# GpSimd widens the quantised rows and multiplies a third lent tile in the gate stage of a quantised feed-forward block

## The reference, cut to what matters

```
def _act_fake_quant(x, clip_factor):
    scale = jax.nn.sigmoid(clip_factor) * jnp.max(jnp.abs(x)) / QMAX
    return jnp.clip(_ste_round(x / scale), -QMAX - 1.0, QMAX) * scale
...
xq = _act_fake_quant(x, clip_x[0])
gate = jnp.einsum('bsh,ih->bsi', xq, _weight_fake_quant(w_gate))
up = jnp.einsum('bsh,ih->bsi', xq, _weight_fake_quant(w_up))
h = _act_fake_quant(jax.nn.silu(gate) * up, clip_down[0])
return jnp.einsum('bsi,hi->bsh', h, _weight_fake_quant(w_down))
```

## Time and profile before

| | before |
|---|---|
| median of 3 runs | 368.54 us (368.09 to 369.57) |
| the profiled execution: time | 369.56 us |
| the profiled execution: span of the trace | 367.8 us |
| TensorE, weight loads, VectorE, ScalarE, GpSimd: busy share of the span | 82%, 64%, 67%, 47%, 39% |
| gate stage, from its first matmul to the last maximum | 274.10 to 324.36 us |

### The profile page before, as it was taken

One profiled execution on the slowest core, in us unless ns is written; L12 is line 12 of the kernel. 1 busy time (PEld: TensorE's weight loads), 2 busy tenths in 40 slices (PEclk: granted clock), 3 DMA queues, 4 the chain that ended last, 5 costly groups with the idle time before them and its releaser, 6 DMA issues.

```text
span 367.8 us, 11114 instructions
## 1 busy us (share of the span) xinstructions
PE 302.9 (82%) x4728; PEld 235.5 (64%) x4734; DVE 247.9 (67%) x489; ACT 173.6 (47%) x286; POOL 145.0 (39%) x138
## 2 busy tenths in 40 slices
PE   6497489779979979979979969969889999717883
PEld 6387469569769769869859858867544333315662
DVE  6956956756646645646645754754337999999995
ACT  6463145336433433442423423322649999559900
POOL 5941883291094094094094050020002133205754
PEclk9676869989989989989969989988979999958897
DMA  4932211501701600601600300301000002002787
GB/s 132 300 120 61 65 55 57 176 4 43 189 4 34 198 4 28 203 4 45 190 4 2 117 4 0 118 4 57 3 0 0 2 0 81 33 2 70 242 255 236
DMA packets 25807, 28.85 MB, mean 78 GB/s; under 512 B 2912, under 2 KB 21664, under 8 KB 25760
## 3 DMA queue, kind: packets, MB, share of 16 engines
q1 hardware_dynamic: 25760, 28.16, 25.0%
HBM read 19.74 MB, written 8.42 MB: 77 GB/s over the span
## 4 chain that ended last, share of the span: by engine, by line
PE 63%; issue 15%; POOL 7%; DVE 6%; ACT 5%; DMA 1%; SPq 1%; POOLq 0%; DVEq 0%; ACTq 0%
PE psum L735 30%; PE psum L994 6%; PE psum L773 5%; PE psum L796 5%; POOL pooled L499 4%; PE psum L757 4%; PE psum L877 4%; PE psum L823 2%; PE psum L806 2%; POOL xT_lo L427 1%; PE psum L832 1%; ACT xq_mem L669 1%; PE psum L839 1%; DMA pooled<-x_dram 1%; ACT silu L681 1%
## 5 line engine op out<-in xcount | busy, mean ns | idle before, releaser
L439 POOL TENSOR_TENSOR xq_mem<-kind,xq_mem 128x256 f32<-128x256 f32 x8 | 4.9, 613 | 110.0 <-DVE arena L1253 109.1
L1166 DVE TENSOR_TENSOR arena<-psum,xq_mem 128x512 f32<-128x512 f32 x64 | 39.7, 682 | 11.2 <-PE psum L757 11.2
L773 PE MATMUL psum<-arena 64*32 64x64 f32 x2048 | 26.2, 240 | 20.4 <-issue 17.8
L994 PE MATMUL psum<-xq_mem,guT 128*128 (+1 forms) x159 | 36.1, 380 | 3.3 <-ACT xq_mem L669 2.5
L489 POOL TENSOR_TENSOR arena<-xin,silu 128x1024 f32 (+2 forms) x7 | 13.2, 1890 | 63.8 <-ACT xin L686 63.8
L773 PEld LDWEIGHTS psum<-arena 64*32 64x32 f32 x2048 | 23.0, 111 | 23.5 <-issue 23.5
L735 PE MATMUL psum<-xT,wT 128*128 128x512 f32 x64 | 33.2, 519 | 2.5 <-ACT xT L573 1.8
L1023 PE MATMUL psum<-dT,arena 128*128 128x256 bf16 x192 | 26.1, 299 | 10.2 <-DVE arena L1378 6.2
L1224 DVE TENSOR_SCALAR psum<-psum 128x64 f32<-128x64 f32 x8 | 1.9, 232 | 46.3 <-PE psum L877 46.3
L735 PE MATMUL psum<-xT,wT_lo 128*128 128x512 f32 x64 | 30.9, 482 | 0.0
L994 PEld LDWEIGHTS psum<-xq_mem,guT 128*128 128x128 bf16 x160 | 14.9, 98 | 24.4 <-issue 3.9
(11 more groups left out here) (218 smaller groups left out, 775.6 us busy)
## 6 DMA issues: line engine op xcount, KB each, us to landing
arena<-in_x SPq DMA_DIRECT2D x8, 512.0 KB, 5.9
x_dram<-arena SPq DMA_DIRECT2D x8, 512.0 KB, 3.6
pooled<-x_dram SPq DMA_DIRECT2D x16, 256.0 KB, 3.1
out<-pooled SPq DMA_DIRECT2D x16, 256.0 KB, 2.5
xin<-in_x_t SPq DMA_DIRECT2D x7, 512.0 KB, 6.3
cs_rows<-cs_dram SPq DMA_DIRECT2D x14, 256.0 KB, 6.0
pooled<-in_w_qkv_t SPq DMA_DIRECT2D x1, 768.0 KB, 5.5
pooled<-in_w_down SPq DMA_DIRECT2D x1, 704.0 KB, 8.8
```

What stands on the lines that cost most here:

```text
L773: last = pe.matmul(Y_BANK[half][b][32 * r:32 * r + 32, at_y:at_y + S], vpad[rows, p, at_v:at_v + 32], dec[rows, c, r, p, odd * S:odd * S + ...
L994: mm = pe.matmul(o[:, 512 * half:512 * half + 512], gT[i][:, c, v * P:v * P + P], xq[:, c, bass.ds(TB * n + 512 * half, 512)], start=(c == ...
L1166: dve.tensor_tensor(dec[:, c, r, :, :], bank[S_BANK[r]].rearrange("q (n k) -> q n k", n=PP), two_heads, ALU.mult).then_inc(dec_done, 1)
```

## The change

`widen_rows` moves from ScalarE to GpSimd, where it is a plain copy from int8 to bf16 of 128 x 1024 values. GpSimd does the first one ahead of the stage's tiles, and in each block but the last one ahead of tile 1 and one ahead of tile 4. ScalarE, which rounds into the slots that GpSimd now reads, gets two waits on `xq_ok`. `LENT` goes from tiles 3 and 5 to tiles 1, 3 and 5, in the last block from tile 3 to tiles 1 and 3. GpSimd's loop over the blocks is written out.

```
--- before.py
+++ after.py
@@ -35,7 +35,7 @@
 NB = TOK // TB
 U = 2 * LAST + 1
 V = LAST + 1
-LENT, LENT_LAST = (3, 5), (3,)
+LENT, LENT_LAST = (1, 3, 5), (1, 3)
 TURN = [2 * i for i in range(LAST)] + [U - 1] + [2 * i + 1 for i in range(LAST)]
 T_HALF = LAST + 1
 T_LENT = (3, 4, 5, 10)
@@ -482,15 +482,22 @@
 
             pool.wait_ge(x1_out, 16 * G)
 
+            def widen_rows(i):
+                pool.wait_ge(q8_ok, i)
+                pool.tensor_copy(xq[:, :, 512 * i:512 * i + 512], q8[:, i % 2, :].rearrange("p (c t) -> p c t", c=DC)).then_inc(xq_ok, 1)
+
             def multiply(n, last):
+                if n == 0:
+                    widen_rows(1)
                 for v in range(V):
+                    if v in (1, 4) and not last:
+                        widen_rows(2 * n + 2 + v // 4)
                     if is_lent(v, last):
                         pool.wait_ge(up_ok, lent(n, v, last))
                         pool.tensor_tensor(hid_step(n, v), up[:, 0:span(v)], silu_2[:, v % 2, 0:span(v)], ALU.mult).then_inc(hl_ok, 1)
 
-            with pool.Fori(0, NB - 1) as n:
-                multiply(n, False)
-            multiply(NB - 1, True)
+            for n in range(NB):
+                multiply(n, n == NB - 1)
 
             def add_up(n, tiles):
                 for j in tiles:
@@ -664,14 +671,8 @@
                 act.activation(q8[:, k, :].rearrange("p (c t) -> p c t", c=DC), pooledT[:, :, bass.ds(512 * i, 512)],
                                ACT.Identity, scale=x_sc[:, 4:5]).then_inc(q8_ok, 1)
 
-            def widen_rows(i, k):
-                act.wait_ge(q8_ok, i)
-                act.activation(xq[:, :, bass.ds(512 * i, 512)], q8[:, k, :].rearrange("p (c t) -> p c t", c=DC),
-                               ACT.Copy).then_inc(xq_ok, 1)
-
             act.wait_ge(xs_ok, 1)
             round_rows(1, 1)
-            widen_rows(1, 1)
 
             def gates(n, first, last):
                 for v in range(V):
@@ -688,13 +689,12 @@
                         if v == 0:
                             if first:
                                 act.wait_ge(xq0_ok, 1)
+                            else:
+                                act.wait_ge(xq_ok, 2 * n)
                             round_rows(2 * n + 2, 0)
-                        elif v == 1:
-                            widen_rows(2 * n + 2, 0)
                         elif v == 3:
+                            act.wait_ge(xq_ok, 2 * n + 1)
                             round_rows(2 * n + 3, 1)
-                        elif v == 4:
-                            widen_rows(2 * n + 3, 1)
 
             gates(0, True, False)
             with act.Fori(1, NB - 1) as n:
```

## The result

Over 16 runs of either kernel the median went from 367.62 us (363.53 to 373.13) to 373.32 us (369.92 to 379.08). The ratio is 1.0156, with a 95% interval of 1.0114 to 1.0199; executions more than 1.5% above the fastest of their kernel are left out of it.

What follows compares the result with a forecast made beforehand. The gate stage, with three nearly full engines, would be bound by the lent odd tiles' shared slot and GpSimd's cast: +8.8 us, plus +2.2 for two clock falls, on the 368.54 us median gives 379.5 us, range 375.0 to 384.5.

Steps and rivals of the forecast that it cites:

- The loop through the odd slot: Gate stage: lent tiles 1, 3, 5 share one silu slot and up buffer; 4.68 us per step against TensorE's 3.46.
- the chain: Gate stage, silu of tile 1 to the next block's: 12.73 us + X, 14.0 for a steady block against 11.55.
- The sum without the clock: Gate stage, all four blocks: +2.7 in block 0, +5.0 in blocks 1 and 2, +1.1 in block 3, together +8.8 us.
- the two falls: Starts of blocks 1 to 3: TensorE's clock drops to 1.2 GHz at two of three, 1.1 us each, +2.2 us.
- The unknown X: Length of GpSimd's cast (row widening), not in the trace: taken as 1.3 us, between a memset's 0.9 and a multiplication's 2.36.
- The step from ScalarE's copy to GpSimd's product: Gate stage, lent tiles: 0.21 us from the end of the copy of up to GpSimd's start.
- The step from the last cast to TensorE's first matmul: Block starts: 0.25 us from the end of GpSimd's widening to TensorE's first matmul of the next block.
- The idle time: TensorE's wait at the start of each later block, put at some 3.2 us with dense work on both sides.
- The clock holds: Rival, block starts: TensorE's clock stays at 1.00 through the waits, only the +8.8 us counts, 377.3 us; chance 0.27.
- The cast is dear: Rival, GpSimd's widening: a cast takes 2.36 us like a product, +5.3 us, 382.6 to 385 us; chance 0.08.
- faster: Rival, gate stage: the odd slot doesn't bind, blocks go from 11.55 to TensorE's 10.4 us, time to 365; chance 0.04.

Runs made afterwards that it cites:

- own_slots: Changed kernel with silu of tiles 1, 3 and 5 in three places and a separate up buffer for tile 3; median 367.09 us, ratio 1.0041.
- widen_only: Changed kernel with the lent tiles of the kernel before (3 and 5, in the last block 3); median 368.31 us, ratio 1.0062.
- cast_twice: Changed kernel with every cast on GpSimd done twice over the same values; median 384.36 us, ratio 1.0501.
- widen_early: widen_only with a block's second rounding behind silu of tile 2 and its cast ahead of GpSimd's multiplication of tile 3; median 365.77 us, ratio 0.9969.
- pool_loop: Changed kernel with GpSimd's work of the first three blocks in a loop again; median 374.21 us, ratio 1.0225.
- after_again: The changed kernel run once more, unaltered; median 374.54 us, ratio 1.0200, gate stage 56.81 us.
- own_slots_early: own_slots with a block's second cast ahead of the multiplication of tile 3, as in widen_early; median 363.96 us, ratio 0.9951.

## Why the prediction was right in kind and too high

**What bounds the stage: right.** The loop through the odd slot is what lengthens the blocks. own_slots takes it away and leaves GpSimd's work as it is, and 6.2 of 6.5 us go. The cast behind the product of tile 3 is on the chain (widen_only, cast_twice) and harmless ahead of it (widen_early).

**The sum without the clock: 8.8 foreseen, 6.5 measured.** This is the step that failed, together with the two falls below: the path was right, and three of its terms were too large.

- The unknown X: taken as 1.3, measured 1.04. It counts four times, and that makes 1.0 us. The row it should have been nearer to was the memset of the earlier trace rows, not the select. The Trainium skill (GPSIMD Engine Reference, 3.1) gives loop bodies of at most two operations 1.03 cycles an element, an estimate of 0.88 us for 1024 values at 1.2 GHz, without the dispatch, for which that section has a figure of VectorE only. The trace's 1.04 agrees with it if the dispatch takes some 0.16.
- The step from ScalarE's copy to GpSimd's product: taken as 0.21 from the kernel before, measured 0.08. The change writes GpSimd's loop out, and pool_loop shows that this is what made the step shorter. There are two such steps on the chain of a block: 0.7 us in the three blocks that pool_loop has in its loop, and some 0.26 in block 3, about 1.0 together. I saw the loop go in GpSimd's list and gave it no price.
- The step from the last cast to TensorE's first matmul: taken as 0.25 at every block, measured 0.05 at the start of block 3, which is 0.2 us. TensorE's own loop holds blocks 1 and 2 only, and block 3 stands behind it. That this is the reason is argued from pool_loop, not tested.

The trace of before had both short steps, ahead of and in its last block, which stands outside the loops of the engines:

```profile
307.97 1.06 ACT L669 ACTIVATE xq_mem<-q 128x1024 int8 x1
...
316.56 1.02 ACT L686 ACTIVATE xin<-psum 128x1024 f32<-128x1024 f32 x1
```

The widening ends at 309.03 and TensorE starts at 309.08; the copy ends at 317.58 and the product starts at 317.65. In after_again the last cast ends at 313.04 and TensorE starts at 313.09:

```profile
312.00 1.04 POOL L487 CAST xq_mem<-q 128x1024 bf16<-128x1024 int8 x1
...
313.09 8.81 PE L994 MATMUL psum<-xq_mem,guT 128*128 128x512 bf16 x40 [2.37 <-POOL xq_mem L487]
```

With X = 1.04 and the step of 0.08 the chain is 12.73 - 0.26 + 1.04 = 13.51 for a steady block, and with the short step at its end 13.31 for block 2; after_again has 13.52 and 13.29.

**The clock: price right, count uncertain.** A fall costs 1.1 to 1.2 us (14.72 and 14.39 against 13.52 and 13.29). I put two falls into the number, and took the case with at most one for the less likely. Of three profiles of the changed kernel two have two falls and one has none, and pool_loop, with waits of 2.5 to 2.7 us, has none either. The idle time was foreseen as 3.2 us and is 2.3 to 2.6, but its length does not decide alone: cast_twice waits 3.60, 3.67 and 3.41 us at its three later starts and has one fall there. So +2.2 belongs to some executions only, and how many isn't shown. The Trainium skill (TensorE: Matmul & The Clock Gate, Part 1) says of the clock's rise at the start of a kernel that it comes after a different number of matmuls in different runs of the same kernel. The falls here vary between profiles of one kernel too, two, none and two, and I should have spread the term over the range.

**The whole time.** The forecast is 6.2 us over the measured 373.32. Of that 0.9 is the median that it started from (368.54 of three executions, 367.62 of 16), 2.3 the chain and 2.2 the two falls; the last 0.8 is what the medians show less than the 6.5 of the stage, and that stays open. The medians of 16 stand 5.7 us apart and the means 6.1 (367.83 and 373.97); the medians of after_again and of the kernel before beside it, 8.0. The part ahead of the stage, which no kernel changes, ended anywhere from 267.2 to 274.2 us; the kernel before has both 267.2 and 274.1, the changed one 270.4, 272.5 and 274.2. So the head start of its first profile was scatter. The interval of the ratio, 1.0114 to 1.0199, holds the 6.5 us (1.018), not the 8.9 (1.024). With such scatter the times can't tell how often the clock falls.

**The range.** Its lower end was the case without a fall with a cast of 0.9 us, 375.7, made from the median of three runs. It left out that steps read from a loop might be shorter outside it (1.2 us), and that this median stood 0.9 us over that of 16 runs. Neither alone would have reached down to where the time lies; both together would.

**The rivals.** "The clock holds" is the nearest, with 377.3: in after_again its mechanism is what happened. "The cast is dear" and "faster" were wrong. What the faster rival said it needed, a loop that doesn't bind, is own_slots_early: 48.18 us, blocks of 10.8 to 11.5 as against TensorE's 10.4.

## What to carry to other kernels

Giving an idle engine more work may cost next to nothing by its sum of busy time (GpSimd had 8 of 13.5 us, and own_slots runs the same work in blocks of 12) and much by its buffers: before lending a tile, count from one use of the slot to the next and compare it with the time that the producer takes for as many tiles. A piece of work that others wait for belongs ahead of a long one that can wait, on an engine that does all in order. And when only one stage is changed, compare its length between profiles; the part ahead of it scatters by 7 us here.

## What the runs showed of the hardware

- GpSimd's cast of 128 x 1024 values from int8 to bf16 took 1.03 to 1.04 us, a little less than ScalarE's 1.05 in the earlier trace rows, while its product of two full inputs took 2.35.
- GpSimd started 0.08 us behind the end of ScalarE's copy where its list was written out, and 0.21 behind it where the same work stood in a loop (after_again and pool_loop). TensorE started 0.25 us behind the end of the rows' widening inside its loop and 0.05 us outside of it, both in the kernel before and in after_again.
- The granted clock fell to its lower level at four of the nine starts of later blocks in the three profiles of the changed kernel, where TensorE had been idle for 2.3 to 2.6 us, and at none of three in pool_loop, after 2.5 to 2.7. In cast_twice it fell towards the end of a wait of 1.39 us at the start of the stage and behind one of 3.67, and not behind waits of 3.60 and 3.41. Each fall cost 1.1 to 1.2 us of the block (changed kernel against after_again).
